# Four graph layers on one core: the gates' tangents by tile during the third pass, with a halved identity on ScalarE and one more subtraction on GpSimd

## The reference

```
h = jnp.maximum(_layernorm(x, axis=-1), 0.0)
x = x + _L1_gnn_ref(h, src, dst, edge_weight, edge_weight_n2, ...)
...
    h = (feat - mean) * jax.lax.rsqrt(var + EPS) * gamma + beta
    feat_in = h @ W_in + b_in
    feat_out = h @ W_out + b_out
    a_in = jax.ops.segment_sum(feat_in[src] * iw[:, None], dst, num_segments=N)
    a_out = jax.ops.segment_sum(feat_out[dst] * ow[:, None], src, num_segments=N)
    a = jnp.concatenate((a_in, a_out), axis=1)
    xi = a @ W_x2i + b_x2i
    hh = h @ W_h2h
    i_i, i_n = jnp.split(xi, 2, axis=1)
    h_i, h_n = jnp.split(hh, 2, axis=1)
    input_gate = jax.nn.sigmoid(i_i + h_i)
    new_gate = jnp.tanh(i_n + h_n)
    h = new_gate + input_gate * (h - new_gate)
```

## Time and profile before

| | us |
|---|---|
| three runs, lowest / median / highest | 3412.09 / 3413.3 / 3416.75 |
| the profiled execution | 3413.15 |
| its span, first to last instruction | 3411.4 |

### The profile page before, as it was taken

How to read it: one execution, slowest core, us unless ns; L and a number is a source line. 1 busy time by engine, 2 the same in 40 slices (tenths; PEclk the granted TensorE clock), 3 DMA queues, 4 the chain that set the end, 5 groups by cost and what they waited for, 6 DMA issues and landing times. The chain is left out here.

```text
span 3411.4 us, 52351 instructions
## 1 busy us (share of the span) xinstructions
PE 2826.2 (83%) x11580; PEld 1817.4 (53%) x11581; DVE 2144.9 (63%) x6395; ACT 1115.9 (33%) x2964; POOL 2361.5 (69%) x2449
## 2 busy tenths in 40 slices
PE   4999877676795788878999887666668999999999
PEld 2444444444454455444333335444445479999998
DVE  7999844344446565556777656444444688888884
ACT  1899700000144000000000004000003567777772
POOL 4777777777777777777777776777772166666662
PEclk6999876767896899989999998777779999999999
DMA  4000033333214334446777773333331357777774
GB/s 152 2 2 2 9 105 104 104 105 104 73 27 158 107 117 126 126 124 191 208 207 208 208 206 108 105 104 105 104 105 37 117 169 212 215 212 214 215 211 147
DMA packets 184390, 439.52 MB, mean 129 GB/s; under 512 B 53944, under 2 KB 78643, under 8 KB 184253
## 3 DMA queue, kind: packets, MB, share of 16 engines
q0 software_dynamic: 135280, 372.30, 37.8%
q1 hardware_dynamic: 48973, 65.58, 5.9%
HBM read 403.39 MB, written 34.22 MB: 128 GB/s over the span
## 5 line engine op out<-in xcount | busy, mean ns | idle before, releaser
L836 POOL DMA_INDIRECT acc<-table,stg_idx x1170 | 1120.4, 958 | 364.8 <-issue 323.9
L2137 PE MATMUL psum<-acc,oh 128*128 x2600 | 938.2, 510 | 412.7 <-SPq L644 150.3
L2137 PEld LDWEIGHTS psum<-acc,oh 128*128 128x128 f32 x2600 | 605.4, 251 | 742.4 <-issue 651.3
L1058 ACT CAST stg_idx<-rec 128x2 int32 (+1 forms) x784 | 149.3, 193 | 1767.2 <-PE psum L2137 1300.6
L1518 DVE TENSOR_TENSOR acc<-acc,psum 128x257 f32 (+1 forms) x660 | 278.8, 422 | 707.5 <-PE psum L2137 693.5
L986 POOL DMA_INDIRECT TT<-qtable,stg_row x440 | 422.1, 959 | 200.0 <-issue 164.0
L862 POOL DMA_INDIRECT H<-gtable,stg_idx x391 | 374.8, 959 | 119.2 <-issue 96.3
L2158 PE MATMUL psum<-H,oh 128*128 x880 | 406.9, 604 | 42.4 <-SPq L654 30.8
L1509 DVE TENSOR_SCALAR oh<-iota,stg_lw 128x128 f32<-128x128 f32 x1320 | 405.8, 363 | 54.4 <-issue 53.1
L2450 PEld LDWEIGHTS psum<-oh,TT 128*128 128x128 f32 x3520 | 426.3, 191 | 19.5 <-issue 0.3
L2450 PE MATMUL psum<-oh,TT 128*128 128x128 f32 x3520 | 427.7, 275 | 0.0
(11 more groups left out here) (272 smaller groups left out, 3089.9 us busy)
## 6 DMA issues: line engine op xcount, KB each, us to landing
acc<-table,stg_idx POOLq DMA_INDIRECT x1173, 2.8
TT<-loc_dram SPq DMA_DIRECT2D x22, 320.0 KB, 5.2
TT<-qtable,stg_row POOLq DMA_INDIRECT x440
Wm<-loc_dram SPq DMA_DIRECT2D x22, 320.0 KB, 4.9
H<-gtable,stg_idx POOLq DMA_INDIRECT x391, 3.7
gtable<-H SPq DMA_DIRECT2D x24, 256.0 KB, 2.1
qtable<-H SPq DMA_DIRECT2D x24, 256.0 KB, 2.2
table<-H SPq DMA_DIRECT2D x8, 640.0 KB
```

The costliest lines, as they stand in the source:

```text
L836: pool.indirect_dma_start(out=dst[:, c, 0:D], out_offset=None, in_=src, in_offset=bass.IndirectOffsetOnAxis(ap=stg_idx[:, c:c + 1], axis=0 ...
L2137: last = mm(sum_bank(j)[:, 0:w], oh[:, 2 * j + k, :], rows_flat[:, ds(start[j] + k * S, w)], start=(k == 0), stop=(k == 1))
```

## The change

The change has four parts, all in the junction but the first.

- VectorE computes, in `sort(1)`, a fourth row of `step_tabs`: `tile_end`, six numbers, the count of `added` at which tiles 0 to 5 have had their last step of the third pass.
- ScalarE loads these six numbers into registers after `gates_kept` has reached its end, and waits before tile n's two tangents for `ended[n]` only. Tile 6 waits for the end of the pass as before.
- `half` is made by ScalarE, after the fourteen tangents, and no longer by VectorE.
- The difference for tile 0 goes to GpSimd as well, so that VectorE's `finish(0)` waits for `gates_less` like the others.

```diff
-        node_tab, wide_slot, gate_tab = [step_tabs[k:k + 1, :] for k in (0, 32, 64)]
+        node_tab, wide_slot, gate_tab, tile_end = [step_tabs[k:k + 1, :] for k in (0, 32, 64, 96)]
...
-            for n in range(1, NT):
+            for n in range(NT):
                 b = blocks_in(n)
                 pool.wait_ge(gates_ready, n + 1)
                 for k in range(2):
                     nc.gpsimd.tensor_tensor(agg[0][:, b, k * P:(k + 1) * P], own_at(k, n), gate_at(2 + k, b),
                                             ALU.subtract).then_inc(gates_less, 1)
...
             act.wait_ge(gates_kept, 2 * UNITS + 1)
-            act.wait_ge(added, 3 * PAIRS + SB)
+            ended = loads(mybir.EngineType.Activation, tile_end, 0, NT - 1, 3 * PAIRS + SB)
 
             for n in range(NT):
+                act.wait_ge(added, ended[n] if n < NT - 1 else 3 * PAIRS + SB)
                 for f, scale, ready in ((1, 1.0, gates_ready), (0, 0.5, sig_ready)):
 
                     at = gates_at[f][:, blocks_in(n), :]
                     nc.scalar.activation(at, at, ACT.Tanh, scale=scale).then_inc(ready, 1)
+            nc.scalar.activation(half, ident[:, :], ACT.Copy, scale=0.5).then_inc(half_made, 1)
...
                 if o == 1:
                     V.tensor_scalar(gate_tab, src[qb, 0:PAIRS], float(D), None, ALU.mult)
+                    V.tensor_scalar(tile_end[:, 0:NT - 1], srt[96:97, 5, TB - 1:NB - 1:TB], float(2 * PAIRS + SB), None, ALU.add)
...
             def finish(n):
 
                 b = blocks_in(n)
-                if n == 0:
-                    dve.wait_ge(gates_ready, 1)
-                    for k in range(2):
-                        last = V.tensor_tensor(agg[0][:, b, k * P:(k + 1) * P], own_at(k, 0), gate_at(2 + k, b), ALU.subtract)
-                    link(last)
                 dve.wait_ge(sig_ready, n + 1)
                 for k in range(2):
-                    if n:
-                        dve.wait_ge(gates_less, 2 * n - 1 + k)
+                    dve.wait_ge(gates_less, 2 * n + 1 + k)
                     t = agg[0][:, b, k * P:(k + 1) * P]
                     last = V.scalar_tensor_tensor(t, gate_at(k, b), 1.0, t, ALU.add, ALU.mult)
                 last.then_inc(gated, 1)
 
-            V.tensor_scalar(half, ident[:, :], 0.5, None, ALU.mult).then_inc(half_made, 1)
```

## The result

The changed kernel takes 3423.3 us (median of 10 runs, 3421.17 to 3424.17) where the one before takes 3412.5 us on the same chip (10 runs): a ratio of 1.0029, 95% interval 1.0021 to 1.0037. Forecast were 3411.3 us and a range up to 3416.0. The profiled execution took 3421.74 us, its span is 3420.0 us. That is 8.6 us more than the profiled execution of before and not 10.8, because its third pass happened to end 2.3 us earlier; in the ten profiled executions of whole kernels here this end lies anywhere from 2045.6 to 2048.3 us, so all comparisons of stages are made from it.

A forecast was written before the change was run, and what follows sets the result against it. Bound: GpSimd's back-to-back fourth-pass gathers, released by the junction's end, ScalarE's packed tail behind TensorE's sums. 3413.15 - 2.2 + 0.2 = 3411.15 us profiled; median 0.15 higher, so 3411.3 us, range 3407.0 to 3416.0.

The forecast's parts named there:

- What bounds it: Fourth pass: GpSimd's gathers run back to back, so what the first gather gains, the end of the pass gains.
- Tangents: ScalarE around the third pass's end: tangents from about 2035.6, free at 2049.1 instead of 2060.45; 11.4 us off ScalarE, not the end.
- `half`: Behind the third pass: moving it from VectorE to ScalarE costs nothing, as TensorE fills itself until about 2049.9.
- TensorE's wait: TensorE's own sums at tile 3: the wait of 0.90 us for GpSimd's sum into x goes, giving 0.9 us.
- the term of the gain: Junction's end: 2.2 us gained, 0.9 from TensorE's wait and 1.3 from the lag that ScalarE had.
- VectorE against GpSimd: After the third pass: finish(0) to (2) pair with GpSimd's subtractions, six pairs at 1.5 us; tile 0's statistics start 1.7 us earlier.
- the rival of nothing left: Junction: blocking falls worse, ScalarE stays behind TensorE, only 0 to 1 us comes through; 3413.0 us, chance 0.17.
- Blocked additions: Third pass's end: VectorE's eight PSUM additions wait for GpSimd, 0.9 us each; 3.9 us on top, 3415.2 us, chance 0.06.
- The table tile_end: At the start: one more VectorE instruction for six numbers, at most 0.39 us, taken as 0.2 us of cost.

The follow-up runs named there:

- e6: The changed kernel, but GpSimd waits before tile 0's subtraction for a count of additions reached some 5 us before the third pass ends; 3410.7 us, ratio 0.9993.
- third bench: A bench by itself, computing no layers: GpSimd's subtractions, mostly directly behind a DMA, with VectorE requests of several kinds; requests took 0.69 to 13.92 us.
- e2: The changed kernel, but all tangents wait for the end of the third pass; 3422.7 us, ratio 1.0029 to the kernel before.
- e1: The changed kernel, but VectorE subtracts for tile 0 again; 3422.0 us, ratio 1.0025 to the kernel before.
- masked change: The changed kernel with the loaded counts in waits masked to 16 bits, as a control; 3422.8 us, ratio 1.0028 to the kernel before.
- e5: The changed kernel, but all tangents wait for the third pass's end and ScalarE makes `half` ahead of them; 3413.9 us, ratio 1.0003 to the kernel before.

## Why the prediction was wrong

- **What bounds it: right.** The junction's shift went through the fourth pass whole, and the medians of the versions follow their junctions within 2 us: 37.8, 39.8, 42.1 and 52 us go with 3408, 3410.5, 3413 and 3423 us.
- **Tangents, `half`, TensorE's wait: right.** ScalarE was free at 2048.3 (the tangents began at 2031.61, 4 us before the time allowed, and the register load doesn't show between them), `half` cost nothing behind early tangents, and e6 gained 2.3 us of junction against 2.2. There TensorE begins the last block 1.2 us sooner after the pass, where 0.9 had been forecast, and the tail behind it is 1.1 us shorter, where 1.3 had been. So the term of the gain was sized well for a kernel in which VectorE and GpSimd take turns; that the two parts miss in opposite ways is luck.
- **VectorE against GpSimd: the step that failed.** The prediction took "six pairs at 1.5 us, until 2057.3" from rows in which GpSimd had started behind a wait and used them for a run that starts directly behind the last gather. It said itself, in the rival of nothing left, that "every estimate above assumes which of two waiting engines goes next", but priced a miss at one sum into x (2.0 us). The miss was ten instructions (12.1 us of one product: 12.79 against 0.69), so TensorE's third product came 10.0 us late, and a low clock of TensorE cost 3.0 us on top, for which the prediction had no term. That the two engines block each other was known; that VectorE can be kept waiting from one GpSimd instruction to the next was not.
- **Blocked additions: right to be small.** The additions from PSUM took 0.41 to 0.42 us beside L951. SBUF — State Buffer of the Trainium skill (Who interferes with whom) says that only instructions with two SBUF inputs or in a two-port mode meet GpSimd's reads; the third bench agrees (0.69 us with one input in PSUM, 11.49 with two in SBUF).
- **The table tile_end: right.** Its instruction took 0.17 us (0.2 in the sum), and the ends were right: twelve tangents before the end of the pass.

When exactly VectorE gets in stays open in part. In most rows of the benches it came in behind GpSimd's last instruction. In the kernel it came in ahead of the last one, on 53 partitions and a quarter as wide as the one ahead (1.08 us, held up by VectorE, where it took 0.63 in the kernel before). Behind a first instruction of 1024 on 16 or 32 partitions it came in ahead of the last of twelve equal ones (1.70 us instead of 1.22), and once at a second gather. Cores out of step may allow the first of these (those without a part in the short one are idle), but it wasn't tried.

## What to carry to other kernels

When work moves to GpSimd, look at what stands directly ahead of it in its queue: behind a DMA that GpSimd issues, or an instruction on fewer partitions and of another length, a run of reads without an unmet wait can keep VectorE's instructions that meet GpSimd's reads (two inputs in SBUF, or an fp32 tensor_scalar or copy there) waiting until it ends or nearly ends. A wait that isn't met yet, 0.3 us of it, or one for GpSimd's own last instruction, ends that. And a row from before prices a conflict only if both engines come to it in the same way; where they don't, the long end of the range is the whole queue of the other engine and not one instruction.

## What was not expected of the hardware

- A request of VectorE for two SBUF inputs, or a tensor_scalar or copy of fp32 in SBUF, took 6.6 to 21.3 us while GpSimd started 4 to 14 further instructions, where it takes 1.4 to 1.8 us when the two take turns; even one of 128x4 took 10.96 us.
- A plain DMA in GpSimd's queue (11.48 us) does what an indirect one does (11.49 us).
- TensorE idle for 9.83 us came back at a granted clock of 0.51 and kept it for 6.0 us, 3.0 us of cost. So it did in e2 after 10.55 us idle, in e1 after 9.51 us (6.1 us at the low clock) and in the masked change after 10.27 us (3.3 us, 1.6 of cost), while in e5, idle for 1.59 us there, it stayed at 1.00.
